# A delta, cross-attention and expert layer on one core: four staging buffers for keys, the second batch's queries made in the delta tail, weight loads and query projection one slot earlier in the cross steps

## What is computed

```python
x = _layernorm(x + attn(x))            # q, k, v by projection, short convolution and silu; delta rule in
                                       # chunks of 32; three FIR paths; a gate mixes 5 paths; output projection
x = _layernorm(x + xattn(x, ctx_1024)) # q_w on x, k_w and v_w on the context, 16 heads of width 16,
                                       # softmax of scores, o_w
x = _layernorm(x + ffn(x))             # top 2 of 8 experts and 2 shared ones, swiglu with hidden width 352
```

## Time and profile before

| | |
|---|---|
| median of 3 runs | 965.95 us (965.72 to 967.9) |
| profiled execution | 968.62 us, of which the span of the trace is 966.8 us |
| busy | PE 830.7 us (86%), DVE 594.1 (61%), ACT 449.3 (46%), POOL 351.1 (36%) |
| chain that ended last | PE 51%, DVE 12%, ACT 11%, DMA 10%, POOL 8%, issue 5% of the span |
| of it, two DMA groups | stores `q_pad<-staged` 4%, strips `queries<-q_pad` 3% |

### The profile page before, as it was taken

One profiled execution on the slowest core, in us unless ns is written; L12 is line 12 of the kernel. 1 busy time (PEld: TensorE's weight loads), 2 busy tenths in 40 slices (PEclk: granted clock), 3 DMA queues, 4 the chain that ended last, 5 costly groups with the idle time before them and its releaser, 6 DMA issues.

```text
span 966.8 us, 17149 instructions
## 1 busy us (share of the span) xinstructions
PE 830.7 (86%) x6187; PEld 615.1 (64%) x6187; DVE 594.1 (61%) x1431; ACT 449.3 (46%) x831; POOL 351.1 (36%) x321
## 2 busy tenths in 40 slices
PE   7799789779989888984677878988988999999895
PEld 5677557667667665773454545556875777777774
DVE  5799899467888889672645656753552333333265
ACT  5687666446665654531244545665322332222221
POOL 9422201024455447432001344334530142222693
PEclk9999999879999997997678889999998999999998
DMA  5699669898967867356234555306303222221421
GB/s 170 194 276 289 207 178 284 274 227 246 254 161 196 235 189 210 129 179 220 85 135 132 178 164 151 130 30 202 83 23 95 67 66 58 65 66 44 149 64 66
DMA packets 160722, 149.18 MB, mean 154 GB/s; under 512 B 92288, under 2 KB 129216, under 8 KB 159360
## 3 DMA queue, kind: packets, MB, share of 16 engines
q1 hardware_dynamic: 157232, 138.72, 49.2%
q0 software_dynamic: 3408, 9.38, 2.6%
HBM read 86.90 MB, written 61.03 MB: 153 GB/s over the span
## 4 chain that ended last, share of the span: by engine, by line
PE 51%; DVE 12%; ACT 11%; DMA 10%; POOL 8%; issue 5%; SPq 2%; POOLq 0%; DVEq 0%; ACTq 0%
PE ps L2729 10%; PE ps L2744 5%; PE ps L665 4%; DMA q_pad<-staged 4%; DMA queries<-q_pad 3%; PE ps L2593 3%; DVE big L1445 2%; POOL hank L344 2%; PE ps L422 2%; POOL kept L2876 2%; PE ps L2031 2%; PE ps L2104 2%; PE ps L1401 2%; POOL hTlo L2663 2%; PE ps L2606 1%
## 5 line engine op out<-in xcount | busy, mean ns | idle before, releaser
L2154 DVE TENSOR_REDUCE cmx<-ps 128x4 f32<-128x1024 f32 x64 | 77.4, 1219 | 56.6 <-PE ps L2104 56.1
L2729 PE MATMUL ps<-wr,xbT 128*128 x312 | 101.1, 467 | 1.8 <-ACT xbT L2765 1.8
L2191 ACT ACTIVATE cross_room<-ps 128x1024 f32<-128x1024 f32 x64 | 65.6, 1025 | 74.5 <-PE ps L2117 69.1
L2818 POOL DMA_INDIRECT y_dram<-yb,dest_row x39 | 37.5, 961 | 132.7 <-DVE dest_row L2794 128.2
L1361 POOL TENSOR_TENSOR st<-st,exponent 128x20 f32<-128x20 f32 x16 | 56.5, 3533 | 63.6 <-DVE st L1336 61.9
L2729 PEld LDWEIGHTS ps<-wr,xbT 128*128 128x128 f32 x312 | 59.9, 193 | 30.5 <-issue 4.2
L549 DVE SCALAR_TENSOR_TENSOR room<-room 128x256 f32<-128x256 f32 x144 | 58.4, 477 | 11.2 <-ACT room L498 11.2
L2803 DVE TENSOR_TENSOR cross_room<-cross_room,ps 128x352 f32<-128x352 f32 x39 | 20.3, 521 | 60.9 <-PE ps L2729 60.9
L2104 PE MATMUL ps<-keys,queries 49*128 49x256 f32 x224 | 31.7, 364 | 28.1 <-DMA queries<-q_pad 21.1
L2773 ACT ACTIVATE cross_room<-ps 128x352 f32<-128x352 f32 x39 | 18.1, 465 | 74.3 <-PE ps L2729 74.3
L2809 DVE TENSOR_SCALAR yb<-ps,weight 128x256 f32<-128x256 f32 x39 | 18.9, 484 | 50.8 <-PE ps L2744 50.8
(11 more groups left out here) (355 smaller groups left out, 2194.0 us busy)
## 6 DMA issues: line engine op xcount, KB each, us to landing
xs_dram<-staged SPq DMA_DIRECT2D x17, 1040.0 KB, 6.6
room<-in_gW SPq DMA_DIRECT2D x8, 1280.0 KB, 7.4
tok_dram<-room SPq DMA_DIRECT2D x8, 768.0 KB, 6.5
fir_dram<-room SPq DMA_DIRECT2D x6, 1024.0 KB, 7.1
paths<-fir_dram SPq DMA_DIRECT2D x48, 128.0 KB, 3.9
keys<-k_pad SPq DMA_DIRECT2D x28, 196.0 KB
queries<-q_pad SPq DMA_DIRECT2D x28, 196.0 KB
xb<-xs_dram SPq DMA_DIRECT2D x39, 130.0 KB, 2.4
```

The costliest lines, as they stand in the source:

```text
L2154: V.tensor_reduce(mx[:, :, half, :, g].rearrange("p t c -> p c t"), ps[:, pair(h), :].rearrange("p c (t k) -> p c t k", t=TT), AX.X, ALU.m ...
L2191: S.activation(pT[g % 2][:, pair(h)].rearrange("p c k t -> p (c k t)"), ps[:, pair(1 - h), :].rearrange("p c n -> p (c n)"), ACT.Exp, scal ...
L2729: m = nc.tensor.matmul(ps[:, 2 * (j % 2) + half, 0:FF], xbT[j % 2][:, k, :], wr[:, bass.ds(e, 1), k, half, :].rearrange("p e n -> p (e n)" ...
```

## The change

In the tail, keys have four staging pairs (`env.key_staged`, index b % 4) in place of two, with four signals for their stores in place of two (`k_out0`, `k_out1`, by `key_out`). Two of the new pairs lie in the paths of batch 6, so keys 1, 2, 5 and 6 wait for that batch's mix. Batch 1's queries are made in the tail as well (pieces X and Q for b = 1, staged in the paths of batch 7), their store to `q_pad` is in the tail, and the meeting waits for it; the first cross step begins with the strips of keys and queries of batch 1. The load of batch 1's tokens moves from step 11 to step 9. The bank strings are rewritten for the new pieces. In the cross steps the second half of the query projection moves from slot 3 to slot 2, the first product with the values from slot 2 to slot 3, and the expert weights are issued right behind the lift of half 1, all of a step at once, instead of in the rounds after the keys' strips.

The diff, without context:

```diff
...
-    hi, lo = env.key_staged[(b + 1) % 2]
-    sp_strips_out(pg, env.k_pad[b], hi, lo, 1, env.kv.k_out[(b + 1) % 2])
+    hi, lo = env.key_staged[b % 4]
+    sp_strips_out(pg, env.k_pad[b], hi, lo, 1, key_out(env, b))
+
+
+def key_out(env, b):
+    return (env.kv.k_out0 + env.kv.k_out1)[b % 4]
...
-            "c0 c2 K1 K2 c5 v4 v5 K7", "c1 x1 v1 v2 K4 K5 v6", "K0 c3 K3 q3 c7 v7", "v0 c4 v3 c6 K6")) for n, name in enumerate(names.split())}
-        x0T, *late = views(flat(paths[2][:].rearrange("p n t d -> p n (t d)")), 0, n_x, "p (k t) -> p k t", 5, k=KT)
-        q0 = late[0:2]
-        env.key_staged = [env.staged, late[2:4]]
+            "c0 c2 K1 K2 c5 v4 v5 v6", "c1 x0 v1 v2 K4 K5 q1", "K0 c3 K3 q0 c7 K6 v7", "v0 c4 v3 c6 x1 K7")) for n, name in enumerate(names.split())}
+        sixth, seventh, (x0T, *late) = (views(flat(t[:].rearrange("p n t d -> p n (t d)")), 0, n_x, "p (k t) -> p k t", NPATH, k=KT) for t in paths)
+        queries = [late[0:2], seventh[0:2]]
+        env.key_staged = [late[2:4], sixth[0:2], sixth[2:4], env.staged]
...
-            sp.wait_ge(kv.k_out[1], 32)
+            sp.wait_ge(key_out(env, 0), 32)
...
-        def sp_query(_):
-            kv_await(sp, "q3")
-            sp_strips_out(pg, env.q_pad[0], *q0, 0, kv.q_out[0])
+        def sp_query(b):
+            kv_await(sp, f"q{b}")
+            sp_strips_out(pg, env.q_pad[b], *queries[b], 0, kv.q_out[b])
...
-        def pe_turn_first(_):
-            pe.wait_ge(kv.x_in0[0], 16)
-            kv_free(pe, "x1")
+        def pe_turn_first(b):
+            pe.wait_ge(kv.x_in0[b], 16)
+            kv_free(pe, f"x{b}")
...
-                    m = nc.tensor.transpose(kv_bank("x1")[:, (c * TT + t) * P:(c * TT + t + 1) * P],
-                                            env.xin[0][:, t, c * P:(c + 1) * P], ident[:])
+                    m = nc.tensor.transpose(kv_bank(f"x{b}")[:, (c * TT + t) * P:(c * TT + t + 1) * P],
+                                            env.xin[b][:, t, c * P:(c + 1) * P], ident[:])
...
-        def pe_first_query(_):
-            kv_await(pe, "x1")
-            kv_free(pe, "q3")
-            pe_heads("q3", env.Ws["q_w"], x0T).then_inc(*s.q0_made.up())
-
-        def act_late(signal_after):
-            act.wait_ge(s.gate_step, 16 * 5 + 12)
-            act.wait_ge(s.mix, 3 * 6)
-            act.wait_ge(*signal_after)
-
-        def act_turn_first(_):
-            act_late((s.x0_turned, 1))
-            S.copy(flat(x0T), kv_bank("x1")).then_inc(*kv_copied("x1").up())
+        def pe_first_query(b):
+            kv_await(pe, f"x{b}")
+            kv_free(pe, f"q{b}")
+            pe_heads(f"q{b}", env.Ws["q_w"], x0T).then_inc(*s.q0_made.up())
+
+        def act_late(b, made):
+            act.wait_ge(s.gate_step, 16 * b + 12)
+            act.wait_ge(s.mix, 3 * (b + 1))
+            act.wait_ge(*made)
+
+        def act_turn_first(b):
+            act_late(5, (s.x0_turned, b + 1))
+            act.wait_ge(s.q0_made, b)
+            S.copy(flat(x0T), kv_bank(f"x{b}")).then_inc(*kv_copied(f"x{b}").up())
...
-        def act_first_query(_):
-            act.wait_ge(s.q0_made, 1)
+        def act_first_query(b):
+            act_late(5 + 2 * b, (s.q0_made, b + 1))
...
-                m = S.activation(q0[0][:, j, :].bitcast(F32R), kv_bank("q3")[:, j * T:(j + 1) * T], ACT.Identity, bias=env.bq[:, j:j + 1])
+                m = S.activation(queries[b][0][:, j, :].bitcast(F32R), kv_bank(f"q{b}")[:, j * T:(j + 1) * T], ACT.Identity, bias=env.bq[:, j:j + 1])
...
-        def dve_first_query(_):
-            dve.wait_ge(s.q0_hi, 1)
-            low_parts(q0[1], q0[0], kv_bank("q3"), env.bq, kv_copied("q3"))
+        def dve_first_query(b):
+            dve.wait_ge(s.q0_hi, b + 1)
+            low_parts(queries[b][1], queries[b][0], kv_bank(f"q{b}"), env.bq, kv_copied(f"q{b}"))
...
-            act_late((s.k_made, b + 1))
+            act_late(6 if b % 4 in (1, 2) else 5, (s.k_made, b + 1))
...
-            act.wait_ge(kv.k_out[(b + 1) % 2], 32 * (b // 2))
+            act.wait_ge(key_out(env, b), 32 * (b // 4))
...
-                m = S.activation(env.key_staged[(b + 1) % 2][0][:, j, :].bitcast(F32R), kv_bank(f"K{b}")[:, j * T:(j + 1) * T],
+                m = S.activation(env.key_staged[b % 4][0][:, j, :].bitcast(F32R), kv_bank(f"K{b}")[:, j * T:(j + 1) * T],
...
-            hi, lo = env.key_staged[(b + 1) % 2]
+            hi, lo = env.key_staged[b % 4]
...
-                     11: rounds({0: ((K, 4),), 1: ((Q, 0),), 2: ((C, 6),), 3: ((K, 5), (C, 7)), 4: ((K, 6),), 5: ((K, 7),)})}
+                     11: rounds({0: ((K, 4),), 1: ((Q, 0),), 2: ((C, 6),), 3: ((K, 5), (C, 7)), 4: ((X, 1), (K, 6)), 5: ((Q, 1),), 6: ((K, 7),)})}
...
-                      11: rounds({0: ((K, 4),), 1: ((Q, 0),), 2: ((C, 6),), 3: ((K, 5), (C, 7)), 4: ((K, 6),), 5: ((K, 7),)})}
+                      11: rounds({0: ((K, 4),), 1: ((Q, 0),), 2: ((C, 6),), 3: ((K, 5), (C, 7)), 4: ((X, 1), (K, 6)), 5: ((Q, 1),), 6: ((K, 7),)})}
...
-                      11: rounds({2: ((v, 4), (Q, 0)), 5: ((v, 5),), 6: ((v, 6),), 7: ((v, 7),)})}
+                      11: rounds({2: ((v, 4), (Q, 0)), 5: ((v, 5),), 6: ((v, 6),), 7: ((Q, 1),), 8: ((v, 7),)})}
...
-                     9: rounds({0: ((C, 0), (C, 1)), 3: ((X, 0), (C, 2), (C, 3))}),
+                     9: rounds({0: ((C, 0), (C, 1)), 3: ((X, 0), (C, 2), (C, 3), (X, 1))}),
...
-                     11: rounds({0: ((out, 3), (first, 0), (X, 1)), 1: ((out, 4), (sp_query, 0)),
-                                 4: ((out, 5), (Q, 0), (out, 6), (out, 7))})}
+                     11: rounds({0: ((out, 3),), 1: ((out, 4), (sp_query, 0), (first, 0)),
+                                 4: ((out, 5), (out, 6), (Q, 0), (sp_query, 1), (out, 7))})}
...
-        pg.meet([env.fir_out, s.cross_in, *s.x1_out, kv.q_out[0], kv.k_out[1]])
+        pg.meet([env.fir_out, s.cross_in, *s.x1_out, *kv.q_out, *(key_out(env, b) for b in range(3))])
...
-        yield
...
-                if 0 <= step - stage < B:
+                if 0 <= step - stage < B and not (stage < 0 and step == 0):
...
-            for _ in range(rounds if b > 1 else 0):
+            for _ in range(rounds):
...
-            if b == 1:
-                copied(sp, "q", b)
-                sp_strips_out(pg, env.q_pad[i], q_hi, q_lo, 0, kv.q_out[i])
-                for half in range(2):
-                    sp_query_in(b, half)
-                sp_tokens_in(2)
...
-            sp.wait_ge(kv.k_out[(b + 1) % 2], 32 * (b // 2 + 1))
+            sp.wait_ge(key_out(env, b), 32 * (b // 4 + 1))
...
+            sp_weights(b)
...
-            yield from sp_weights(b)
...
-            if b == B:
+            if b in (1, B):
...
-            for j in range(KT):
-                for k in range(KT):
-                    m = nc.tensor.matmul(bank("q", b)[:, j * T:(j + 1) * T], Ws["q_w"][:, k, j * P:(j + 1) * P], xT[:, k, :],
-                                         start=(k == 0), stop=(k == 1))
-                if j == 0:
-                    yield from later(b, 1)
-            m.then_inc(*s.q_made.up())
+            pe_query_half(b, 0)
...
+        def pe_query_half(b, j):
+            for k in range(KT):
+                m = nc.tensor.matmul(bank("q", b)[:, j * T:(j + 1) * T], Ws["q_w"][:, k, j * P:(j + 1) * P], xT[:, k, :],
+                                     start=(k == 0), stop=(k == 1))
+            if j == 1:
+                m.then_inc(*s.q_made.up())
+
...
-            if b == B:
+            if b in (1, B):
...
-            act.wait_ge(s.x_turned, b)
-            act.wait_ge(s.q_made, b - 1)
+            act.wait_ge(s.x_turned, b - 1)
+            act.wait_ge(s.q_made, b - 2)
...
-            act.wait_ge(s.q_made, b)
-            act.wait_ge(kv.k_out[0], 32 * B // 2)
+            act.wait_ge(s.q_made, b - 1)
+            act.wait_ge(key_out(env, B - 1), 32 * B // 4)
...
-            if b == B:
+            if b in (1, B):
...
-            dve.wait_ge(s.q_hi, b)
+            dve.wait_ge(s.q_hi, b - 1)
...
-            pool.wait_ge(s.x_turned, b)
+            pool.wait_ge(s.x_turned, b - 1)
...
-        AT = {2: 0, 5: 1, 6: 2, SLOTS: 3}
+        AT = {3: 0, 5: 1, 6: 2, SLOTS: 3}
...
+                if slot == 2 and b + 2 < B:
+                    pe_query_half(b + 2, 1)
...
-                yield
...
-                for _ in sp_routed_up(e):
-                    pass
+                sp_routed_up(e)
...
-                yield from sp_routed_up(b)
+                sp_routed_up(b)
...
-                yield from sp_shared_weights(pg, a, env, 0)
+                sp_shared_weights(pg, a, env, 0)
...
-                yield from sp_routed_up(b - 1)
+                sp_routed_up(b - 1)
...
+                sp_query_in(1, half)
+            sp_tokens_in(2)
...
-                    all_units(sp_shared_weights(pg, a, env, 1))
+                    sp_shared_weights(pg, a, env, 1)
...
-        env.kv = pg.signals("KeysValues", "", "x_in0 x_in1 k_out q_out strips_in0 strips_in1")
```

(1 more changed line is left out.)

## The result

| | before | after |
|---|---|---|
| median of the runs | 966.92 us (965.72 to 975.44, 4 runs) | 941.18 us (932.90 to 944.34, 4 runs) |
| ratio, 95% interval | | 0.9702 (0.9618 to 0.9786) |
| profiled execution, span | 968.62 us, 966.8 us | 944.34 us, 942.5 us |

The kernel became 26 us faster by these medians; the forecast was 27.6 us. Two more comparisons on other chips gave 0.9713 (0.9682 to 0.9744) and 0.9659 (0.9602 to 0.9715). A kernel's executions fall now and then into a slower state, and every ratio here is taken from the other ones; two of the six runs of e7, its profiled one among them, were slow.

What follows compares the result with a forecast made beforehand. Bound taken: each cross step's ring of query projection, staging, store to `q_pad`, strips read back, first scores. 16.4 + 3.0 + 3.5 + 4.7 = 27.6 us off 965.95 gave 938.4 us; range 930 to 950, to hold 0.8.

Steps and rivals of the forecast that it cites:

- Rival A: Cross steps: starts at 2.4 GHz bring 2 us per step instead of 0.7, meeting doesn't move; 931 us; chance 0.2.
- signs named ahead: Cross steps: stores 3 to 4.5 us, first waits under 2, scores about 6.1 behind lift, steps 21 to 23, clock above 0.9.
- the 454: Tail: the meeting was expected at 450 to 452 us; one behind 454 would show the forecast wrong.
- Part 1: Cross steps: weights behind the lift of half 1 free the query store, and the lift of half 0 limits next; 16.4 us.
- Rival B: Cross steps: keys' strips, not weights, slow the store, which stays at 7 to 8 us; 955 us; chance 0.1.
- C: Cross steps: moved weights only move the crowd, half the weights' gain is lost, meeting at 453.6; 949 us; chance 0.12.
- Part 3: Cross-step starts: shorter PE gaps keep TensorE's clock up; 0.7 us in five steps, 3.5 us in all.
- Part 2: Cross steps: second half of the projection one slot earlier; 0.5 us in six steps, 3.0 us in all.
- Part 4: Tail: making batch 1's queries there gains 5.5 us before the first reduction, meeting loses 0.8; net 4.7 us.
- Part 5: Tail: with four key buffers, keys 1 wait for batch 6's mix with 2.6 us margin; cost nothing.
- Rival D: Cross steps: slower, PE waits at slot 4 for the lift of half 1 in steps loading weights; 973 us; chance 0.03.

Runs made afterwards that it cites:

- e7: Kernel after, with the expert weights issued right behind the query store instead of seven us in front of it; 944.10 us, ratio 0.9677.
- e1: Kernel before, with only the expert weights moved right behind the lift of half 1; 947.36 us, ratio 0.9775.
- e3: Kernel after, with the expert weights put back in front of the query store; 960.38 us, ratio 0.9908.
- e8: Kernel after, with the query strips of half 0 issued ahead of the lift of half 0; 943.05 us, ratio 0.9678.
- e6: Kernel before, with eight unread matmuls added at the end of each of the first five attended steps; 964.72 us, ratio 0.9911.
- e4: Kernel after run again unchanged, for its spread; 943.00 us, ratio 0.9713.
- e9: Kernel after run again unchanged, as same-chip partner of a version with query strips ahead of the lift; 938.84 us, ratio 0.9659.
- e5: Kernel after, with the projection's second half and the product with the values back in their old slots; 947.89 us, ratio 0.9726.
- e2: Kernel after, with weights and projection's second half put back, leaving only the tail's changes; 964.99 us, ratio 0.9950.

## Why the prediction was right, and where its terms were off

The forecast of 938.4 us and the median of 941.18 differ by less than the kernel's spread; as a gain, 27.6 us were forecast, and the medians give 25.7 to 33.0 in the three comparisons. The shape was right: no rival but a part of A came true. That the sum fits as closely as it does is in part luck, since the clock was priced too low and the projection probably too high.

Of the signs named ahead, the stores, the waits and the distance from the lift came out. The steps should have lasted 21 to 23 us, and three of five lie outside (19.55, 24.14, 20.53); the clock should have been above 0.9 in every start, and was 0.50 in one. The meeting stands at 461.1 us, behind the 454 that was to show the forecast wrong. But 9.8 us of that delay lie ahead of the landmark; counted from there the meeting moved by 1.0 us, which would put it at 451.3 in the trace before.

**Part 1, weights.** The mechanism held: e1, e3 and e7 show it from three sides. The store was priced at 3.0 us and took 3.4 and 4.1. The next limit was named rightly: the first scores follow the lift by 6.72, 6.53, 6.53, 6.62 and 5.82 us where 6.11 was assumed, and e8 shows that the lift is the limit. Only at the first start, whose gain was counted like the others, is it still the store. The Trainium skill, "DMA: Bandwidth & Descriptors", section "Queues, rings and completion order", says that on one engine descriptors of a queue are taken in ring order; the stores of e3 and e7 (7.1 and 4.3 us) agree. Rival B is out by the store's time, C by e1: moving the weights returned no crowd.

**Part 3, clock.** This term was mis-sized: "I take 0.7 us in five steps". e6 gives at least some 2.0 us a step. The busy times by stretch in the trace after:

```profile
514.20:519.60 5.40, 5.37 (x22) 2.98 (x22) 1.91 (x3) 1.63 (x3) 1.46 (x2) 0.50 0.48 160
...
560.30:565.70 5.40, 5.39 (x40) 3.61 (x40) 3.65 (x7) 3.24 (x5) 4.32 (x5) 1.00 0.60 202
```

The second step alone began at 1.2 GHz, after a wait of 1.93 us, and lasted 24.14 us; in e4 and e9 it began so too and lasted 22.90 and 24.23. In e1 and e5 the same step followed the same wait (1.94, 1.91 us), began at 0.50 us for the first scores, which is full clock, and lasted 21.46 and 21.39. So a cold start costs that step some 1.4 to 2.8 us, if the small differences between these kernels are left aside. Rival A's value was about the right one, in four of five steps; parts 1 and 3 together, forecast at 19.9 us, measured 24.8 in e1. My reason for the reduced value, short waits for DVE and ACT, was no measure of it.

**Part 2, projection.** Forecast 3.0 us; 3.9 to 4.9 where the weights stay, and with them moved 1 to 3 by e5, which is not shown to differ from nothing. That it shrinks once the store has left the ring was the forecast's own argument. The stretch agrees: e1 gained 24.8 us and e2 4.5 in its tail, 29.3 together, and the whole change 29.8, so little is left for part 2.

**Part 4, tail.** The meeting moved by 1.0 us (forecast 0.8), the awaited store took 8.74 us (bound 8.6), the reduction follows by 2.0 (2.0): net 4.4 us against 4.7. e2's ratio, 0.5%, agrees.

**Part 5.** From batch 4's mixing product to the landmark, e2 and e3, whose tails have four key buffers and the mix to wait for, take 68.2 us each; e1 and e6, whose tails are the old ones, take 68.2 and 67.6: the wait for batch 6's mix costs nothing that can be seen.

Rival D didn't happen; in the steps with weights no wait for a lift is in the chain after.

## What to carry to other kernels

On one queue, bulk loads issued right ahead of a transfer on the critical ring lengthened it here by 3 us, and issued right behind it by nearly nothing; but what comes next on the ring may then pay, as e7's first step did. Issued 5 us ahead they cost nothing that can be seen. When a wait in a ring goes, the clock that the wait had cost comes back as well; price it by a filled gap, not by a guess. And where the untouched part of a kernel varies by 10 us between traces, measure from a landmark late in that part.

## What the runs showed of the hardware that I hadn't expected

Eight useless matmuls in each of five gaps made the kernel 0.9% faster (e6), with the granted clock over the steps' first 5.4 us at 1.00 instead of 0.50 to 0.68 and the stores as slow as before. Nearly the same wait was followed by a start at 1.2 GHz in four traces (1.80 to 1.95 us in after, e4, e7 and e9, first scores 0.78 to 0.80 us), by one at 2.4 GHz that lasted in two (1.91 and 1.94 us in e5 and e1, first scores 0.50 us, 1.00 over 5.4 us), and in e3 by one at 2.4 GHz that fell within those 5.4 us (1.80 us, 0.68). What decides between them is open. And the same code took from 348.6 to 358.8 us up to batch 4's mixing product over the twelve traces, in part at a granted clock of 0.51 in one trace and 1.00 in another over the same 16 us.
